# Spreading the normalisation over two engines at both ends, and an inverse root on ScalarE, in a group normalisation with a circular depthwise convolution

## What is computed

```python
x_cat = jnp.concatenate([x, x[:, :, :-1, :]], axis=2)
out = jax.lax.conv_general_dilated(x_cat, weight, window_strides=(1, 1), padding='VALID',
        dimension_numbers=('NCHW', 'OIHW', 'NCHW'), feature_group_count=x.shape[1])
return out + bias[None, :, None, None]
...
m = jnp.mean(g, axis=(2, 3, 4), keepdims=True)
s = jnp.var(g, axis=(2, 3, 4), keepdims=True)
return ((g - m) / jnp.sqrt(s + eps)).reshape(v.shape)
...
x = x + _L0_conv_ref(_gn(x), L0_conv_weight, L0_conv_bias)
```

## Time and profile before

| | |
|---|---|
| median of 3 runs | 801.14 us |
| the profiled execution | 799.6 us |
| its span | 797.8 us |
| busy: TensorE, VectorE, ScalarE, GpSimd | 690.0, 713.8, 673.1, 583.9 us |
| moved | 316.09 MB, mean 396 GB/s |
| TensorE's granted clock, mean | 0.998 |

### The profile page before, as it was taken

How to read it: one execution, slowest core, us unless ns; L and a number is a source line. 1 busy time by engine, 2 the same in 40 slices (tenths; PEclk the granted TensorE clock), 3 DMA queues, 4 the chain that set the end, 5 groups by cost and what they waited for, 6 DMA issues and landing times.

```text
span 797.8 us, 9115 instructions
## 1 busy us (share of the span) xinstructions
PE 690.0 (86%) x1920; PEld 557.9 (70%) x1920; DVE 713.8 (89%) x1602; ACT 673.1 (84%) x1029; POOL 583.9 (73%) x1110
## 2 busy tenths in 40 slices
PE   0599999898899888998988998888898989988895
PEld 0477877776677667776776777777776767776784
DVE  7899999998998899999989999999888999989962
ACT  6799998888889888898888898888887888897893
POOL 4688787777677667687777677677786777776775
PEclk9999999999999999999999999999999999999999
DMA  9979999999999999999999999999999999999956
GB/s 343 409 301 375 410 410 418 424 418 417 416 416 414 414 426 412 413 404 402 405 417 418 412 402 400 411 412 410 402 409 406 409 407 399 410 406 403 375 239 251
DMA packets 43784, 316.09 MB, mean 396 GB/s; under 512 B 12816, under 2 KB 12944, under 8 KB 14992
## 3 DMA queue, kind: packets, MB, share of 16 engines
q1 hardware_dynamic: 43728, 315.51, 97.4%
HBM read 161.32 MB, written 154.14 MB: 395 GB/s over the span
## 4 chain that ended last, share of the span: by engine, by line
DMA 41%; SPq 16%; DVE 16%; POOL 10%; ACT 8%; issue 6%; PE 2%; POOLq 0%
DMA xt<-x 29%; DVE st L311 9%; DMA out<-xt 8%; SPq L190 7%; SPq L172 7%; POOL xt L278 6%; ACT xn L387 6%; DVE xt L336 4%; DMA runs<-taps 3%; ACT kept L396 2%; PE conv L462 2%; DVE runs L320 1%; DMA xt<-wide 1%; SPq L179 1%; SPq L183 1%
## 5 line engine op out<-in xcount | busy, mean ns | idle before, releaser
L462 PE MATMUL conv<-xn,runs 128*128 128x448 f32 x1536 | 645.3, 567 | 38.4 <-ACT xn L387 36.7
L462 PEld LDWEIGHTS conv<-xn,runs 128*128 128x128 f32 x1536 | 514.1, 346 | 101.9 <-ACT xn L387 58.5
L278 POOL TENSOR_TENSOR xt<-xt,kept 128x448 f32<-128x448 f32 x384 | 436.7, 1144 | 97.8 <-ACT kept L396 97.4
L387 ACT ACTIVATE xn<-xt,shift,rstd 128x672 f32<-128x672 f32 x512 | 462.8, 942 | 44.6 <-POOL shift L272 44.6
L311 DVE BATCH_NORM_STATS2 st<-xt 128x6 f32<-128x336 f32 x1024 | 451.9, 494 | 54.1 <-DMA xt<-x 49.4
L336 DVE SCALAR_TENSOR_TENSOR xt<-conv,bias_all,xt 128x448 f32<-128x448 f32 x384 | 256.8, 669 | 18.0 <-PE conv L462 18.0
L396 ACT ACTIVATE kept<-conv,bias_all 128x448 f32<-128x448 f32 x384 | 234.2, 620 | 10.7 <-PE conv L462 9.8
L438 PEld LDWEIGHTS p_mean<-msum,neg_mean 128*128 128x128 f32 x128 | 19.5, 192 | 94.3 <-POOL msum L247 79.5
L438 PE MATMUL p_mean<-msum,neg_mean 128*128 128x8 f32 x128 | 25.2, 269 | 59.2 <-POOL msum L247 59.2
L377 ACT ACTIVATE std<-var,eps 128x8 f32<-128x8 f32 x64 | 19.3, 301 | 54.5 <-DVE var L326 54.0
L268 POOL TENSOR_TENSOR newt<-r 128x8 f32<-128x8 f32 x64 | 12.7, 198 | 49.9 <-DVE r L331 48.2
(11 more groups left out here) (29 smaller groups left out, 111.6 us busy)
## 6 DMA issues: line engine op xcount, KB each, us to landing
xt<-x SPq DMA_DIRECT2D x128, 672.0 KB, 7.5
out<-xt SPq DMA_DIRECT2D x128, 672.0 KB, 6.8
xt<-x SPq DMA_DIRECT2D x128, 336.0 KB, 7.6
out<-xt SPq DMA_DIRECT2D x128, 336.0 KB, 6.9
out<-xt SPq DMA_DIRECT2D x128, 168.0 KB, 12.0
xt<-x SPq DMA_DIRECT2D x124, 168.0 KB, 12.4
runs<-taps SPq DMA_DIRECT2D x32, 192.0 KB, 10.9
xt<-wide SPq DMA_DIRECT2D x4, 336.0 KB, 7.2
```

The source lines that it names most:

```text
L278: nc.gpsimd.tensor_tensor(cell, cell, kept_of(u, c), ALU.add).then_inc(pool_added, 1)
L387: ins = nc.scalar.activation(xn[:, n % NS, :, part], xt[0:P, n % XS, :, part], ACT.Identity, scale=rstd[:, n % RS, b:b + 1], bias=shift[:, ...
L462: nc.tensor.matmul(bank(c), lay[:, :, c], channel_of(xn, u % NS, c), start=True, stop=True).then_inc(conv_ready, 1)
```

## The change

- *Batches.* ScalarE normalises only five of the eight batches of units 0, 1, 62 and 63. The other three are done by GpSimd for units 0 and 1 (for unit 0 right after its coefficients, for unit 1 one after each of the first three additions of unit 0), and by VectorE for units 62 and 63 (after the first addition of the unit before).
- *Root.* ScalarE computes the inverse root at once with `Abs_reciprocal_sqrt` in place of `Sqrt`, and VectorE's reciprocal is gone.
- *Statistics.* VectorE takes a unit's 16 statistics four later than before; the last four stand between the additions of the next unit. At the start there are 38 before the loop, in place of 48, and 18 and 20 in units 0 and 1.
- *Places.* A table says after which step each of the small steps comes; units 0 and 1 have their own. The zeroing of slot 5 comes before the loop's prologue on GpSimd.

```diff
@@ -57,6 +57,18 @@
+LATE = 4
+ACT_BATCHES = 5
+POOL_HELPED = (0, 1)
+DVE_HELPED = (UNITS - 2, UNITS - 1)
+USUAL = {"sums": 0, "mean": 4, "negmean": 2, "deviations": 1, "variance": 6, "add_vars": 3, "root": 3, "newton": 2}
+AT_START = ({"sums": 3, "mean": 8, "negmean": 5, "deviations": 4, "variance": 11, "add_vars": 5, "root": 5, "newton": 5},
+            {"sums": 1, "mean": 5, "negmean": 3, "deviations": 2, "variance": 8, "add_vars": 4, "root": 4, "newton": 3})
 
 DVE_CH = (0, 2, 4, 6, 8, 10)
 ACT_CH = (1, 3, 5, 7, 9, 11)
@@ -75,6 +87,10 @@
 def through(channels, u, c):
 
     return u * len(channels) + sum(k <= c for k in channels)
+
+
+def place(step, u):
+    return (AT_START[u] if u < len(AT_START) else USUAL)[step]
 
 
 def build(nc, x, wide, taps, bias, out):
...
@@ -237,6 +253,7 @@
             nc.gpsimd.memset(three_halves[:], 1.5).then_inc(consts_set, 1)
             pool.wait_ge(consts_set, 2)
             nc.gpsimd.memset(xt[:, 4, :, :], 0.0).then_inc(slot_zeroed[4], 1)
+            nc.gpsimd.memset(xt[:, 5, :, :], 0.0).then_inc(slot_zeroed[5], 1)
 
             def add_means(n):
                 r = n % RS
@@ -272,6 +289,12 @@
                 nc.gpsimd.tensor_tensor(shift[:, r, :], nmean[:, r, :], rstd[:, r, :], ALU.mult
                                         ).then_inc(coef_ready, 1)
 
+            def normalize(n, b):
+                pool.wait_ge(coef_ready, n + 1)
+                part = slice(b * ROW, (b + 1) * ROW)
+                nc.gpsimd.tensor_scalar(xn[:, n % NS, :, part], xt[0:P, n % XS, :, part], rstd[:, n % RS, b:b + 1],
+                                        shift[:, n % RS, b:b + 1], ALU.mult, ALU.add).then_inc(pool_normed, 1)
+
             def add_x(u, c):
                 pool.wait_ge(act_evicted, through(ACT_CH, u, c))
                 cell = channel_of(xt, u % XS, c)
@@ -281,36 +304,46 @@
                 add_means(n)
                 deviations(n)
                 newton(n)
-            add_means(LEAD_COEF)
-            nc.gpsimd.memset(xt[:, 5, :, :], 0.0).then_inc(slot_zeroed[5], 1)
+                if n == 0:
+                    for b in range(ACT_BATCHES, BP):
+                        normalize(0, b)
 
             for u in range(UNITS):
                 n = u + LEAD_COEF
-                add_x(u, ACT_CH[0])
-                if n < UNITS:
-                    deviations(n)
-                for c in ACT_CH[1:4]:
+                for k, c in enumerate(ACT_CH):
                     add_x(u, c)
-                if n < UNITS:
-                    newton(n)
-                add_x(u, ACT_CH[4])
-                if n + 1 < UNITS:
-                    add_means(n + 1)
-                add_x(u, ACT_CH[5])
+                    if u == 0 and ACT_BATCHES + k < BP:
+                        normalize(1, ACT_BATCHES + k)
+                    if n < UNITS:
+                        if k == place("sums", u):
+                            add_means(n)
+                        if k == place("deviations", u):
+                            deviations(n)
+                        if k == place("newton", u):
+                            newton(n)
 
         @block.vector
         def _(dve):
             nc.vector.memset(eps[:], EPS).then_inc(consts_set, 1)
             nc.vector.memset(runs[:], 0.0).then_inc(runs_zeroed, 1)
 
-            def stats(n, k0, k1):
-                for k in range(k0, k1):
-                    h, b = k // BP, k % BP
+            def stats(first, last):
+
+                for at in range(first, min(last, UNITS * HALVES * BP)):
+                    n, h, b = at // (HALVES * BP), at // BP % HALVES, at % BP
                     if b == 0:
                         dve.wait_ge(x_loaded[n % XS][h], 16 * len(PIECES) * (n // XS + 1))
                     ins = nc.vector.bn_stats(st[:, n % RS, h, b, :], xt[0:P, n % XS, h, b * ROW:(b + 1) * ROW])
-                if k1 == HALVES * BP:
-                    ins.then_inc(stats_ready, 1)
+                    if h == HALVES - 1 and b == BP - 1:
+                        ins.then_inc(stats_ready, 1)
+
+            def normalize(n, b0, b1):
+                dve.wait_ge(coef_ready, n + 1)
+                dve.wait_ge(conv_ready, (n - NS + 1) * CG)
+                for b in range(b0, b1):
+                    part = slice(b * ROW, (b + 1) * ROW)
+                    nc.vector.tensor_scalar(xn[:, n % NS, :, part], xt[0:P, n % XS, :, part], rstd[:, n % RS, b:b + 1],
+                                            shift[:, n % RS, b:b + 1], ALU.mult, ALU.add).then_inc(dve_normed, 1)
 
             def lay_out(g):
 
@@ -326,10 +359,6 @@
                 nc.vector.tensor_reduce(var[:, n % RS, :], parts.rearrange("k (h b e) -> k b h e", h=HALVES, b=BP),
                                         AXIS.XY, ALU.add).then_inc(var_ready, 1)
 
-            def invert(n):
-                dve.wait_ge(std_ready, n + 1)
-                nc.vector.reciprocal(r0[:, n % RS, :], std[:, n % RS, :]).then_inc(r0_ready, 1)
-
             def take(u, c):
                 dve.wait_ge(conv_ready, u * CG + c + 1)
                 cell = channel_of(xt, u % XS, c)
@@ -337,33 +366,31 @@
                                                op0=ALU.add, op1=ALU.add).then_inc(dve_taken, 1)
 
             ALL = HALVES * BP
-            stats(0, 0, ALL)
-            stats(1, 0, ALL // 2)
+            stats(0, ALL * 3 // 2)
             add_vars(0)
-            stats(1, ALL // 2, ALL * 3 // 4)
-            invert(0)
-            stats(1, ALL * 3 // 4, ALL)
+            stats(ALL * 3 // 2, ALL * 2)
             lay_out(0)
-            stats(2, 0, ALL // 2)
+            stats(ALL * 2, ALL * 2 + 6)
             add_vars(1)
-            stats(2, ALL // 2, ALL * 3 // 4)
-            invert(1)
-            stats(2, ALL * 3 // 4, ALL)
 
             dve.wait_ge(bias_loaded, 16)
-            ends = (3, 6, 8, 11, 13, 16)
+            ends = (0, 3, 6, 8, 11, 13, 16)
+            at_start = ((38, 41, 44, 47, 50, 53, 56), (56, 60, 64, 68, 72, 74, 76))
             for u in range(UNITS):
+                begin = (u + LEAD_STATS) * ALL - LATE
+                parts = at_start[u] if u < len(at_start) else [begin + e for e in ends]
                 for k, c in enumerate(DVE_CH):
-                    if u + LEAD_STATS < UNITS:
-                        stats(u + LEAD_STATS, ends[k - 1] if k else 0, ends[k])
+                    if u < UNITS - LEAD_STATS:
+                        stats(parts[k], parts[k + 1])
                     take(u, c)
                     if k == 1 and u % PER_GROUP == PER_GROUP - 1 and u + 1 < UNITS:
                         lay_out((u + 1) // PER_GROUP)
-                    if u + LEAD_COEF < UNITS:
-                        if k == 3:
-                            add_vars(u + LEAD_COEF)
-                        if k == 4:
-                            invert(u + LEAD_COEF)
+                    if u + LEAD_COEF < UNITS and k == place("add_vars", u):
+                        add_vars(u + LEAD_COEF)
+                    if u + LEAD_NORM in DVE_HELPED and k == 0:
+                        normalize(u + LEAD_NORM, ACT_BATCHES, BP)
+                if u == UNITS - 1 - LEAD_STATS:
+                    stats(begin + ALL, UNITS * ALL)
 
         @block.scalar
         def _(act):
@@ -374,10 +401,15 @@
 
             def root(n):
                 act.wait_ge(var_ready, n + 1)
-                nc.scalar.activation(std[:, n % RS, :], var[:, n % RS, :], ACT.Sqrt, bias=eps[:, 0:1]
-                                     ).then_inc(std_ready, 1)
+                nc.scalar.activation(r0[:, n % RS, :], var[:, n % RS, :], ACT.Abs_reciprocal_sqrt, bias=eps[:, 0:1]
+                                     ).then_inc(r0_ready, 1)
+
+            def batches(n):
+                return ACT_BATCHES if n in POOL_HELPED + DVE_HELPED else BP
 
             def normalize(n, b0, b1):
+                if n >= UNITS or b0 >= batches(n):
+                    return
                 if b0 == 0:
                     act.wait_ge(coef_ready, n + 1)
                     if n >= NS:
@@ -386,7 +418,7 @@
                     part = slice(b * ROW, (b + 1) * ROW)
                     ins = nc.scalar.activation(xn[:, n % NS, :, part], xt[0:P, n % XS, :, part], ACT.Identity,
                                                scale=rstd[:, n % RS, b:b + 1], bias=shift[:, n % RS, b:b + 1])
-                if b1 == BP:
+                if b1 == batches(n):
                     ins.then_inc(norm_ready, 1)
 
             def evict(u, c):
@@ -399,37 +431,25 @@
             for n in (2, 3):
                 nc.scalar.memzero(xt[:, n, :, :]).then_inc(slot_zeroed[n], 1)
             act.wait_ge(consts_set, 2)
-            nc.scalar.activation(warm[:], eps[:], ACT.Sqrt)
+            nc.scalar.activation(warm[:], eps[:], ACT.Abs_reciprocal_sqrt)
             negmean(0)
             root(0)
+            normalize(0, 0, 3)
             negmean(1)
-            normalize(0, 0, 2)
+            normalize(0, 3, ACT_BATCHES)
             root(1)
```

(35 more changed lines are left out.)

## The result

The changed kernel takes 806.12 us (median of 20 runs, 802.39 to 810.92), the kernel before 800.3 (20 runs): a ratio of 1.0069, interval 1.0052 to 1.0086. It is slower, by 0.7 per cent, which is clear of the noise; I had said 796.0 and named 802.5 as the upper end. The profiled execution took 809.1 us with a span of 807.2.

What follows compares the result with a forecast made beforehand. Transfers were taken to bound the middle, compute the ends. Start 0.5, middle 1.5 and end 3.0 made 5.0 us off the profiled 799.6, 794.6; with the median 1.5 higher, 796.0 was forecast, range 789.5 to 802.5.

Steps and rivals of the forecast that it cites:

- What bounds the kernel: Whole kernel: transfers fill the DMA engines in the middle, 11.99 us a unit; only the two ends are not full.
- The middle's 1.5 us: Middle units: stores ready earlier, 1 per cent of SP's 148.5 us of waits reaches the end; 8 gained to 3 lost.
- The start: First 60 us: earlier first convolution mostly given back by late sums; 0.5 us gained, from 1.6 gained to 5 lost.
- The unused transfers: Start: idle transfer time stays almost whole, moved to about 47.5 to 51.5 us, 4.0 us instead of 4.5.
- GpSimd's batch: Units 0 and 1: one normalising batch on GpSimd takes 0.75 us, between its memset's and its add's scaled prices.
- VectorE's batch: Units 62 and 63: one normalising batch on VectorE charged 1.0 us, bounds 0.45 and 1.5.
- Rival A: Start: GpSimd's batch costs like its add, 1.72 us, so the start loses 5 us: 801.6; chance 0.17.
- The end: Last units: earlier coefficients and three batches on VectorE gain 3.0 us, bounds 1.5 and 4.5.
- The cycle in the usual order: Compute per unit with the usual places: some 11.2 us instead of 11.05, under 11.99 and hidden by transfers.
- The slower rival, C: Middle: compute cycle becomes the bound, above 11.99; at 12.2 us the kernel takes 810; chance 0.10.
- the two new waits: Start: TensorE stands 3 us in unit 0 and waits again in unit 1, each time for late sums.

Runs made afterwards that it cites:

- Experiment 2: The changed kernel with 4 and 6 unused matmuls on TensorE ahead of its waits for the means of units 2 and 3: 801.49 us, 1.0009.
- experiment 6: The changed kernel without GpSimd's batches, ScalarE normalising all eight of units 0 and 1: 807.53 us, 1.0083.
- experiment 9: The changed kernel without GpSimd's batches and with all 48 statistics before the loop, its own places for units 0 and 1 kept: 807.35 us, 1.0094.
- experiment 1: The changed kernel without its own start: usual places from unit 0, 48 statistics before the loop, no GpSimd batches: 796.82 us, 0.9957.
- experiment 12: The changed kernel with usual places from unit 0, GpSimd's batches for unit 0 alone and no late statistics: 798.32 us, 0.9951.
- experiment 4: The kernel before with one edit, VectorE doing three of the eight batches of units 62 and 63: 800.46 us, 0.9989.
- 11: The changed kernel with usual places from unit 0, 48 statistics before the loop, GpSimd's batches for unit 0 alone, none on VectorE: 795.68 us, 0.9937.
- experiment 3: The changed kernel with the copy of the taps behind the fifth addition of its unit, not the second: 805.48 us, 1.0058.

## Why the prediction was wrong

- **What bounds the kernel**: right. Transfers set the middle, and nearly all that differs comes from the two ends. The middle's 1.5 us ("SP's waits shrink") did not come: 415 and 405 GB/s in the hundreds where the earlier trace rows has 417 and 407.
- **The start is the step that failed**: "The idle time stays almost whole, only at another place: 4.0 instead of 4.5", 0.5 us gained, and behind coef(3) "From there the transfers are filling". The unused time was not 0.5 us less but 5.8 more, half of it behind 60 us, where the forecast had none. The first half of the step held: the first convolution goes at 25.62 (24.9 forecast), mean(2) waits 2.94 us (3 forecast). Three things then came out otherwise.
  - *The clock.* I priced the three channels behind mean(2) at 0.75 us each. Behind the idle time they take 4.86 us. So coefficients 2 come at 47.0, not 43.1, and again in unit 1 (4.38 us idle, then 4.64): coefficients 3 at 62.1, not 55.2. Yet the earlier trace rows had a price for this: six matmuls took 4.10 us behind an idle time of 5.96, with the column at 1.00. The column tells nothing there, as the trace's record of the clock begins only at 33.75 us (30.75 in the changed kernel), and until then the convolutions start 0.75 us apart instead of 0.38. A forecast that puts a 3 us hole into TensorE has to price what follows it. Experiment 2 puts this at 5 us.
  - *The places.* I laid the late sums at the door of the seven pieces on GpSimd. Experiments 6 and 9 show that the sums come late without the pieces too: behind the fourth addition they wait for the eviction of channel 7, and TensorE is through with channel 8 by then. I had taken the new table as given and never asked what the usual one would do there; experiments 9 and 1, which differ in it alone, are 11 us apart (1.0094, 0.9957).
  - *The unused transfers.* I took the gap as almost fixed. It is not: it ranged from 0.4 us (experiment 12) to 11.5.
- **GpSimd's batch**: 0.75 forecast (0.57 and 1.72 the bounds), six of them took 950 ns on average (five 902 to 912, one 1167). VectorE's batch: 1.0 charged, 1079 ns on average. Groups of the changed kernel (busy us, mean ns):

```profile
L345 DVE TENSOR_SCALAR xn<-xt,rstd,shift 128x672 f32<-128x672 f32 x6 | 6.2, 1079 | 0.0
L295 POOL TENSOR_SCALAR xn<-xt,rstd,shift 128x672 f32<-128x672 f32 x6 | 5.7, 950 | 0.1
```

  The estimate from the Trainium skill's price of a one-input operation (GPSIMD Engine Reference, Elementwise — side-by-side cycle accounting), about 0.65, is a third too low by this row. Rival A, the batch at the price of an add (1.72), did not happen. Its time, 801.6, was exceeded for another reason.
- **The end**: 3.0 us forecast ("ScalarE had all eight"). The size did not hold, and the direction is not shown by the times: 1 us in experiment 4 and 2 in *11*, both inside the noise, and 0.9 in TensorE's last convolutions. Whether the end of the changed kernel is shorter than before its trace does not show: 47.7 us from the last load's issue, before 46.2, where six other versions with the same end took 46.0 to 47.7. The cycle in the usual order was to be 11.2; it was 11.6 (763.45 to 775.06), since the sums stand behind four additions that have piled up on GpSimd:

```profile
763.45 0.39 PE L458 MATMUL p_mean<-msum,neg_mean 128*128 128x8 f32 x2 [1.30 <-POOL msum L264]
...
775.06 0.39 PE L458 MATMUL p_mean<-msum,neg_mean 128*128 128x8 f32 x2 [1.35 <-POOL msum L264]
777.65 22.25 PE L486 MATMUL conv<-xn,runs 128*128 128x448 f32 x58
```

  The last row shows the part that worked: units 62 and 63 follow without a gap, where the kernel before had 0.93 us. But TensorE now waits 1.30 and 1.35 us for the sums, where it waited 0.70 and 0.56, and all of this comes 8 us later, because the last load is issued at 752.2, not 744.3.
- **The slower rival, C**: it named the middle, whose cycle stayed under 11.99. Rival A lost at the start, but by the batch's price; none of my rivals had the start slow by the places or by the clock, though the forecast had put the two new waits there itself.

What stays open: how the 3.4 us of experiment 1 divide between the late statistics, the usual places and the end; which steps of the table for units 0 and 1 cost most; where the 2 us went that the middle of the changed kernel's profile took longer; and why the rate falls from 415 to 405 GB/s in the later hundreds of nearly every version.

## What to carry to other kernels

When a forecast puts a hole of some microseconds into TensorE, read the granted clock as a cost of its own: the work behind the hole may run at half speed, and a few matmuls of filling show what that is worth. A step's place in an engine's order has to be checked against when its input and its reader are ready, with the old place as the alternative; here the usual places in the first two units, which put the sums behind the first addition and not the fourth, were worth more than all the moved work. Where transfers bound the middle, count the unused transfer time at the ends: it put these fourteen versions roughly in the order of their times. Before a difference of one profile is put down to an edit, look at how much versions with the same code differ there: the last 47 us did by 1.7.

## What the runs showed of the hardware

- TensorE's granted clock fell to 0.50 behind idle times of 2.94 and 4.38 us (changed kernel), where six matmuls of 128x448 then took 4.86 and 4.64 us; behind 3.61 (experiment 6) and 3.62 (experiment 9), where they took 4.86 and 4.22; behind 2.69 (experiment 3), 3.93; and behind 1.69 (experiment 12), where four took 2.87 instead of 1.90. Behind 2.67 and 2.37 (experiments 6 and 9) six took 2.65, at a clock of 1.00. So the length of the one idle time did not decide it. With matmuls in the hole it stayed at 1.00.
- GpSimd's multiply-add of 128 x 672 fp32 with two scalars per partition took 0.95 us on average, 1.41 ns an element, where its addition of two tensors takes 2.55 (1143 ns for 448). VectorE's price for the same batch hangs on GpSimd: in experiment 4 the six ranged from 618 to 1449 ns, with 646 in the middle, the long ones beside GpSimd's additions, of which three took 3.88 us where three alone take 3.35. Both engines pay.
- An inverse root on ScalarE took 0.296 us for 128 x 8, the price of the root it replaced (0.301), with two table loads before the first unit and none behind them, as in the kernel before.
